# Attention and feed-forward: products with V in other places of a batch's second group, and zero products in the last two batches

## The chip, the cores and the metric

The kernel runs on one core of a Trainium2 chip. The time is device microseconds of one execution, and the number compared is the median of several. Five engines work side by side: TensorE (PE; its weight loads are PEld), VectorE (DVE), ScalarE (ACT), GpSimd (POOL) and SyncE (SP), which here only issues DMAs. Each runs its own list of instructions in order and waits on semaphores for the others. TensorE's clock has two levels, 2.4 GHz and 1.2 GHz; the profile gives what was granted as a share, 1.00 or 0.50.

## The reference

A post-norm transformer block over x of 8 batches, 512 tokens, 128 channels, fp32:

```python
qkv = x @ w_qkv                      # (8, 512, 384); 16 heads of 8 channels
att = einsum('bhtd,bhsd->bhts', q, k) / sqrt(8)
att = softmax(where(causal, att, -inf))
x = layernorm(x + einsum('bhts,bhsd->bhtd', att, v))
h = silu(x @ wg.T) * (x @ wu.T)      # 384 hidden, weights are integers / 127
x = layernorm(x + h @ wd.T)
```

## The kernel before, in words

The work has an attention stage, up to about 320 us, and a feed-forward stage behind it, which the change does not touch.

**Groups.** The attention stage runs over 32 groups of four heads, four groups a batch, numbered G = 0 to 31. TensorE's list is written out by hand: `group0` to `group3`, called for G = 4b+1 to 4b+4. So `group1`, the "second group" of batch b in this text, holds G = 4b+2. Three groups are in flight in each of these functions:

- `scores(G, s)`, five steps: K times Q for keys at or before the query, into one of two pairs of PSUM banks (line 449, 35 rows of the array). ScalarE takes each pair away with one exp (`exp_slot`, line 707) into `pt`, GpSimd clears the part above the diagonal (line 935).
- `maxima(M, k)`, for the group M = G + 2, two steps at a time, k = 0, 2, 4, 6, 8: Q times K into one of three banks (line 466, 33 rows), from which VectorE takes each row's maximum (line 792). GpSimd splits these (line 923), `turn_negmax` transposes them (line 431), ScalarE copies them, a DMA puts them beside Q.
- `values(V, ...)`, for the group V = G - 1: the exps times V, in five pieces (line 489). The products are fp32 with all 128 rows of the array and 32 of its columns, four heads one after the other into the four quarters of bank `pv_ps`. A piece is named by its block of keys: "0a" and "0b" are 256 queries each, "1" is 384, "2" is 256, "3" is 128. One piece is four products in the code and eight records in the profile. Two groups share the bank; when the second is complete, ScalarE copies it to `oT` (`copy_out`, line 721), and `turn_out` transposes it in the next group.

**Projections.** Batch b + 2's projections of q and k (line 405, 512 columns, fp32) stand in `group1`, b + 1's projection of V (line 421) in `group0`. They use the same two pairs of PSUM banks as the scores. ScalarE copies their results (`copy_q_or_k`, line 686), GpSimd splits them, and DMAs lay them out for the scores of a later batch. So `group1` of batches 6 and 7 has no projection of q and k, and `group0` of batch 7 none of V.

**Order of the banks.** `SCORE_TURNS` and `MAXIMA_TURNS` list who takes a pair or a bank in turn; a step waits until the one two (or three) turns before it has been read.

**Zeros.** `keep_busy(n)` runs n products of a tile of zeros, bf16, 512 columns (line 498), into `pv_ps` while nothing is in it, in the start of the kernel alone.

Of the kernel before, what the change touches and what calls it, by code (L numbers as in the profile page):

```python
# [32 lines left out]
P = 128  # L33
B, T, C = 8, 512, 128
# [91 lines left out]
def attention_ffn(nc, x, w_qkv, w_gate, w_up, w_down, out):  # L126
    ctx = ExitStack()
    with ctx:
        def sb(name, shape, dt):
            return ctx.enter_context(nc.sbuf_tensor(name, shape, dt))  # L130
# [7 lines left out]
        pv_ps = psum[:, 7, :]  # L138
# [18 lines left out]
        zeros = sb("zeros", [P, T], BF16)  # L157
# [225 lines left out]
        def _(pe):  # L383
# [23 lines left out]
            def project_q(b):  # L407
                if b < B:
                    project(b, 0, take_pair("Q", b)[:, 0, :])
# [5 lines left out]
            def project_v(b):  # L415

                if b < B:
                    pair = take_pair("VX", b)
                    pe.wait_ge(xt_copied, b + 1)
                    for n in range(NB):  # L420
                        last = pe.matmul(pair[:, 0, C * n:C * n + C], xT[:, P * n:P * n + P], wqkv[:, 2 * C:3 * C],  # L421
                                         start=True, stop=True)
                    last.then_inc(v_made, 1)
                    if b + 1 < B:
                        turn_x(b + 1, pair[:, 1, :])
# [29 lines left out]
            def maxima(M, k):  # L455

                if M < GROUPS:
                    u, g = M // NG % 2, M % NG
                    if k == 0:
                        pe.wait_ge(qk_loaded[u][g], LOADED * (M // NG // 2 + 1))  # L460
                    for k in (k, k + 1):
                        bank, at = take_bank("M", M, k), 64 * (k % 2)
                        blocks = max_blocks(k)
                        for n, (hh, i, col) in enumerate(blocks):
                            width = P * (i + 1)
                            last = pe.matmul(bank[:, col:col + width],  # L466
                                             qx[u][at:at + KM, 2 * g + hh // 2, P * i:P * i + P].bitcast(F32R),
                                             kx[u][at:at + KM, 2 * g + hh // 2, 0:width].bitcast(F32R),
                                             start=(n == 0), stop=(n == len(blocks) - 1), skip_group_check=True)
                        last.then_inc(mx_full, 1)  # L470

            def values(G, *pieces):


                u, g = G // NG % 2, G % NG
                half, par = g // 2, g % 2
                for piece in pieces:
                    j = int(piece[0])
                    first, last_q = (0, 256) if piece[1:2] == "a" else (256, T) if piece[1:2] == "b" else (P * j, T)
                    if piece == "0a":  # L480
                        if g == 0:
                            pe.wait_ge(v_copied, G // NG + 1)
                        if par == 0 and G > 1:
                            pe.wait_ge(ot_copied, G // 2)
                    pe.wait_ge(diag_done, NB * G + (1, 2, 4, 3)[j])
                    for hh in range(HG):
                        bank, col = key_block_place(hh, j)
                        at = (j * H + 8 * half + 2 * hh + par) * VW + (VW // 2) * (1 - par)
                        last = pe.matmul(pv_ps[VW * hh:VW * hh + VW, first:last_q], vx[u][:, at:at + VW],  # L489
                                         pt[g % 2][:, bank, col + first - P * j:col + last_q - P * j],  # L490
                                         start=(piece == "0a" and par == 0), stop=False, skip_group_check=True)
                    last.then_inc(pv_piece, 1)

            def keep_busy(n):


                for _ in range(n):
                    pe.matmul(pv_ps, zeros[:, 0:P], zeros[:], start=True, stop=True, skip_group_check=True)  # L498

            def first_maxima(M):  # L500
                for k in range(0, MX, 2):
                    maxima(M, k)
                    if M > 0 and k == 0:
                        turn_negmax(0)
                    keep_busy(3)
# [11 lines left out]
            def group0(G):  # L517
                V, M, b = G - 1, G + LAG, G // NG
                scores(G, 0)
                scores(G, 1)  # L520
                values(V, "0a")
                maxima(M, 0)
                values(V, "1", "0b")
                turn_negmax(G + 1)
                maxima(M, 2)
                scores(G, 2)
                turn_out(half_of(G))
                scores(G, 3)
                maxima(M, 4)
                values(V, "2", "3")  # L530
                scores(G, 4)
                maxima(M, 6)
                project_v(b + 1)
                maxima(M, 8)

            def group1(G):
                V, M, b = G - 1, G + LAG, G // NG
                values(V, "0a")
                scores(G, 0)
                scores(G, 1)  # L540
                maxima(M, 0)
                values(V, "1", "0b", "2")
                maxima(M, 2)
                turn_negmax(G + 1)
                scores(G, 2)
                values(V, "3")
                maxima(M, 4)
                scores(G, 3)
                maxima(M, 6)
                project_q(b + 2)  # L550
                scores(G, 4)
                maxima(M, 8)
                project_k(b + 2)

# [112 lines left out]
        def _(act):  # L667
# [34 lines left out]
            def exp_slot(G, s):  # L702
                if G < GROUPS:
                    act.wait_ge(st_full, SLOTS * G + s + 1)
                    if G > 1:
                        act.wait_ge(pv_piece, PIECES * (G - 2) + pieces_read(G - 2, s))
                    act.activation(pt[G % 2][:, 2 * s:2 * s + 2, :], pair_of("S", G, s), ACT.Exp,  # L707
                                   scale=SM_SCALE).then_inc(exp_done, 1)
# [26 lines left out]
            for G in range(GROUPS + 1):  # L735
                b, n = (G - 1) // NG, (G - 1) % NG
                exp_slot(G, 0)
                exp_slot(G, 1)
                copy_negmax(G + 1)
                exp_slot(G, 2)  # L740
                if n == 1:
                    copy_out((G - 2) // 2)
                exp_slot(G, 3)
                if n == 1 and G > 0:
                    copy_q_or_k(b + 2, 0)
                exp_slot(G, 4)
                if n == 0:
                    copy_v_and_x(b + 1)
                if n == 1:
                    copy_q_or_k(b + 2, 1)  # L750
                if n == 3 and G > 0:
                    copy_out((G - 2) // 2)
# [285 lines left out]
```

## Time and profile before

| | us |
|---|---|
| median of 3 runs | 402.44 |
| the three runs | 421.72, 396.28, 402.44 |
| the profiled execution's own time | 399.73 |
| its span, first to last instruction | 398.0 |
| mean granted clock of TensorE in it | 0.888 |
| TensorE busy | 361.3 (91%) |
| VectorE busy | 290.0 (73%) |
| ScalarE busy | 215.1 (54%) |
| GpSimd busy | 186.6 (47%) |

The profile is of one execution, and its times are set against 399.73, not against the median. A busy share says how long an engine had an instruction in it; a matmul at the lower clock is busy for longer with the same work, so busy time and clock have to be read together.

### The profile page before, as it was taken

How to read it: one execution, taken by the hardware profiler on the slowest of the kernel's cores; microseconds unless marked ns; L12 is line 12 of the kernel's file. 1: busy time of each engine (PE TensorE's matmuls, PEld its weight loads, DVE VectorE, ACT ScalarE, POOL GpSimd, SP SyncE). 2: the span in 40 equal slices, each digit the busy share in tenths (PEclk: the TensorE clock that was granted, in tenths of full speed). 3: DMA queues.
4: the chain of work that ended last, by engine and by line, in shares of the span. 5: the costliest groups of instructions: out<-in, count | busy, mean ns of one | idle time of the engine just before them, and what ended most of it. 6: DMA issues, size and time to landing. Idle time of an engine off the chain costs nothing.

```text
span 398.0 us, 9029 instructions
## 1 busy us (share of the span) xinstructions
PE 361.3 (91%) x2900; PEld 207.4 (52%) x2900; DVE 290.0 (73%) x1239; ACT 215.1 (54%) x277; POOL 186.6 (47%) x349
## 2 busy tenths in 40 slices
PE   5598999999999999999999999999999869788781
PEld 3233465446556445555565564565455437667661
DVE  6777656798898745788888988898587125776751
ACT  3301636586876644667868767776476733332220
POOL 8300312644553461247445525644234455787854
PEclk9969558799999755899999999999599787999998
DMA  5895301174156214433641661543000000001001
GB/s 161 276 321 169 107 3 55 50 259 126 54 217 200 68 62 155 118 119 112 222 132 30 237 194 31 212 152 94 3 4 4 28 2 0 28 28 53 28 27 54
DMA packets 33903, 41.74 MB, mean 105 GB/s; under 512 B 3136, under 2 KB 17472, under 8 KB 33856
## 3 DMA queue, kind: packets, MB, share of 16 engines
q1 hardware_dynamic: 33856, 41.17, 31.8%
q8 instruction: 23, 0.38, 0.4%
q14 instruction: 24, 0.20, 0.2%
HBM read 21.76 MB, written 18.87 MB: 102 GB/s over the span
## 4 chain that ended last, share of the span: by engine, by line
PE 71%; DVE 10%; POOL 6%; issue 6%; DMA 3%; ACT 2%; SPq 0%; POOLq 0%; DVEq 0%; ACTq 0%
PE psum L489 21%; PE psum L466 17%; PE psum L449 13%; PE psum L405 5%; PE psum L396 4%; DVE masked L792 4%; POOL x L994 3%; PE psum L498 2%; PE psum L431 2%; PE psum L421 2%; PE psum L648 2%; POOL rstd L983 2%; DVE stats L846 2%; DMA scr_k<-parts 1%; DVE nm L792 1%
## 5 line engine op out<-in xcount | busy, mean ns | idle before, releaser
L792 DVE CUSTOM_DVE_ANT_0 masked<-psum,mask 128x384 bf16<-128x384 f32 (+3 forms) x512 | 219.7, 487 | 57.7 <-PE psum L466 49.9
L707 ACT ACTIVATE pt<-psum 128x1024 f32<-128x1024 f32 x160 | 158.6, 1022 | 67.3 <-PE psum L449 66.4
L935 POOL TENSOR_SCALAR_AFFINE_SELECT pt<-pt 128x512 f32<-128x512 f32 x128 | 79.6, 634 | 125.7 <-ACT pt L707 124.2
L466 PE MATMUL psum<-kx,qx 33*128 33x384 f32 (+3 forms) x512 | 100.8, 383 | 6.4 <-DMA kx<-scr_k 2.9
L489 PE MATMUL psum<-pt,vx 128*32 128x256 f32 (+2 forms) x1280 | 100.8, 424 | 0.3 <-POOL pt L935 0.3
L449 PE MATMUL psum<-qx,kx 35*128 35x384 f32 (+3 forms) x512 | 83.5, 375 | 1.3 <-ACT pt L707 1.3
L466 PEld LDWEIGHTS psum<-kx,qx 33*128 33x128 f32 x512 | 58.7, 206 | 47.2 <-DVE nm L792 22.5
L449 PEld LDWEIGHTS psum<-qx,kx 35*128 35x128 f32 x512 | 51.4, 209 | 34.5 <-issue 20.9
L489 PEld LDWEIGHTS psum<-pt,vx 128*32 128x32 f32 x1280 | 32.9, 115 | 42.9 <-issue 29.4
L792 DVE DVE_READ_ACCUMULATOR2_ANT nm<- 128x1 f32 x512 | 42.5, 83 | 0.0
L923 POOL TENSOR_SCALAR nm_parts<-nm 128x16 fp32r<-128x16 f32 x32 | 6.6, 206 | 55.2 <-DVE nm L792 54.5
L766 ACT ACTIVATE sg<-psum 128x512 f32<-128x512 f32 x24 | 14.3, 596 | 29.4 <-PE psum L639 28.6
L715 ACT ACTIVATE nm_T<-psum 32x128 f32<-32x128 f32 x32 | 8.5, 266 | 35.9 <-PE psum L431 35.9
L648 PE MATMUL psum<-wT,pt 128*128 128x128 f32 x192 | 22.9, 276 | 1.5 <-DVE pt L881 1.5
L648 PEld LDWEIGHTS psum<-wT,pt 128*128 128x128 f32 x192 | 22.5, 192 | 2.8 <-DVE pt L881 2.3
L405 PE MATMUL psum<-xT,wqkv 128*128 128x512 f32 x32 | 22.2, 796 | 1.6 <-ACT xT L674 1.6
L636 PE MATMUL psum<-x_hi,wT 128*128 128x512 f32 x48 | 22.0, 459 | 0.7 <-ACT x_hi L758 0.7
L639 PE MATMUL psum<-x_lo,wT 128*128 128x512 f32 x48 | 21.0, 437 | 1.7 <-DVE x_lo L862 1.7
L881 DVE TENSOR_TENSOR pt<-psum,sg 128x512 f32<-128x512 f32 x24 | 16.0, 670 | 3.6 <-PE psum L639 2.8
L983 POOL TENSOR_TENSOR rstd<-veps,minus_half 128x4 f32<-128x4 f32 x16 | 16.1, 1009 | 0.0
L954 POOL TENSOR_TENSOR parts<-full,parts 128x512 fp32r<-128x512 f32 x12 | 15.4, 1283 | 1.0
L1005 POOL TENSOR_SCALAR yo<-r,minus_mean,rstd 128x128 f32<-128x128 f32 x32 | 13.9, 448 | 2.0 <-POOL rstd L983 2.0
(60 smaller groups left out, 272.5 us busy)
## 6 DMA issues: line engine op xcount, KB each, us to landing
scr_q<-parts SPq DMA_DIRECT2D x16, 512.0 KB, 3.6
scr_k<-parts SPq DMA_DIRECT2D x16, 512.0 KB, 5.4
qx<-scr_q SPq DMA_DIRECT2D x64, 128.0 KB, 2.5
kx<-scr_k SPq DMA_DIRECT2D x64, 128.0 KB, 2.6
xa<-L_attn_x SPq DMA_DIRECT2D x8, 256.0 KB, 3.2
res<-L_attn_x SPq DMA_DIRECT2D x8, 256.0 KB, 2.7
out<-yo SPq DMA_DIRECT2D x8, 256.0 KB, 2.2
qx<-nm_T SPq DMA_DIRECT2D x64, 8.0 KB
```

Source lines behind the costliest of these rows:

```text
L405: pe.matmul(dst, wqkv[:, C * n:C * n + C], xT[:], start=True, stop=True).then_inc((q_made, k_made)[n], 1)
L449: last = pe.matmul(pair[:, bank % 2, col:col + width], kx[u][at:at + KS, 2 * g + hh // 2, P * j:P * j + P].bitcast(F32R), qx[u][at:at + KS ...
L466: last = pe.matmul(bank[:, col:col + width], qx[u][at:at + KM, 2 * g + hh // 2, P * i:P * i + P].bitcast(F32R), kx[u][at:at + KM, 2 * g + ...
L489: last = pe.matmul(pv_ps[VW * hh:VW * hh + VW, first:last_q], vx[u][:, at:at + VW], pt[g % 2][:, bank, col + first - P * j:col + last_q - ...
L636: pe.matmul(psum[:, bank + k % 2, :], w, x1_hi[u][:].bitcast(F32R), start=True, stop=False)
L639: pe.matmul(psum[:, bank + k % 2, :], w, x1_lo[u][:].bitcast(F32R), start=False, stop=True).then_inc(full, 1)
L648: last = pe.matmul(psum[:, 5, C * n:C * n + C], hid[u][:, m, P * n:P * n + P], wT[:, 2, P * m:P * m + P], start=(m == 0 and n == 0), stop= ...
L707: act.activation(pt[G % 2][:, 2 * s:2 * s + 2, :], pair_of("S", G, s), ACT.Exp, scale=SM_SCALE).then_inc(exp_done, 1)
L792: dve.tensor_tensor_reduce(masked[count % 4][:, 0:width], bank[:, col:col + width], mask[:, T - width:T], -1.0, 3.0e38, ALU.add, ALU.min, ...
L881: dve.tensor_tensor(hid[u][:, m, :], psum[:, 3 + k % 2, :], sg[k % 2][:], ALU.mult).then_inc(hid_made, 1)
L935: pool.affine_select(out=blocks, in_=blocks, pattern=[[0, HG], [1, P]], compare_op=ALU.is_ge, fill=0.0, base=0, channel_multiplier=-1).the ...
L983: pool.tensor_tensor(rstd[:, k, :], veps[:, k, :], minus_half[:], ALU.pow).then_inc(rstd_made, 1)
```

## The change

In `group1`, piece "2" of the products with V no longer follows piece "0b" at once but stands behind `scores(G, 2)`, and piece "3" moves from there to behind `scores(G, 3)`. ScalarE's copy of the completed sums moves behind the exp of step 3 to match. In batch 6, whose `group1` has no projection, piece "3" stands behind `scores(G, 4)` and the copy behind the exp of step 4; four products of zeros are added to the open sums of `pv_ps` behind `maxima(M, 6)`. In `group0` of batch 7, which has no projection of V, four more stand behind `maxima(M, 6)`. They are written with start and stop off, so they add nothing to what is in the bank. No product of the computation is dropped or added.

```diff
--- before.py
+++ after.py
@@ -497,6 +497,11 @@
                 for _ in range(n):
                     pe.matmul(pv_ps, zeros[:, 0:P], zeros[:], start=True, stop=True, skip_group_check=True)
 
+            def add_zeros(n):
+
+                for _ in range(n):
+                    pe.matmul(pv_ps, zeros[:, 0:P], zeros[:], start=False, stop=False, skip_group_check=True)
+
             def first_maxima(M):
                 for k in range(0, MX, 2):
                     maxima(M, k)
@@ -530,6 +535,8 @@
                 values(V, "2", "3")
                 scores(G, 4)
                 maxima(M, 6)
+                if b + 1 == B:
+                    add_zeros(4)
                 project_v(b + 1)
                 maxima(M, 8)
 
@@ -539,16 +546,23 @@
                 scores(G, 0)
                 scores(G, 1)
                 maxima(M, 0)
-                values(V, "1", "0b", "2")
+                values(V, "1", "0b")
                 maxima(M, 2)
                 turn_negmax(G + 1)
                 scores(G, 2)
-                values(V, "3")
+                values(V, "2")
                 maxima(M, 4)
                 scores(G, 3)
-                maxima(M, 6)
-                project_q(b + 2)
-                scores(G, 4)
+                if b + 2 == B:
+                    maxima(M, 6)
+                    add_zeros(4)
+                    scores(G, 4)
+                    values(V, "3")
+                else:
+                    values(V, "3")
+                    maxima(M, 6)
+                    project_q(b + 2)
+                    scores(G, 4)
                 maxima(M, 8)
                 project_k(b + 2)
 
@@ -738,12 +752,14 @@
                 exp_slot(G, 1)
                 copy_negmax(G + 1)
                 exp_slot(G, 2)
-                if n == 1:
+                exp_slot(G, 3)
+                if n == 1 and b + 2 != B:
                     copy_out((G - 2) // 2)
-                exp_slot(G, 3)
                 if n == 1 and G > 0:
                     copy_q_or_k(b + 2, 0)
                 exp_slot(G, 4)
+                if n == 1 and b + 2 == B:
+                    copy_out((G - 2) // 2)
                 if n == 0:
                     copy_v_and_x(b + 1)
                 if n == 1:
```

TensorE, `group1` of batches 0 to 5, before. L489 with 32x384 is piece "1", with 32x256 x8 pieces "0b" and "2", with 32x128 piece "3"; L466 are maxima, L449 scores, L431 the transposed maxima, L405 the projection of q:

```order
L489 MATMUL psum<-pt,vx 32x384 x4
L489 MATMUL psum<-pt,vx 32x256 x8
L466 MATMUL psum<-kx,qx 128x512 x2
L431 MATMUL psum<-identf,nm_parts 128x128
L449 MATMUL psum<-qx,kx 128x384
...
L489 MATMUL psum<-pt,vx 32x128 x4
L466 MATMUL psum<-kx,qx 128x384
...
L449 MATMUL psum<-qx,kx 128x384
...
L466 MATMUL psum<-kx,qx 128x384
...
L405 MATMUL psum<-xT,wqkv 128x512
```

Pieces "1", "0b" and "2" stand in one burst, and the single piece "3" in all that follows up to the projection. The same place in TensorE's list now:

```order
L489 MATMUL psum<-pt,vx 32x384 x4
L489 MATMUL psum<-pt,vx 32x256 x4
L466 MATMUL psum<-kx,qx 128x512 x2
L431 MATMUL psum<-identf,nm_parts 128x128
L449 MATMUL psum<-qx,kx 128x384
...
L489 MATMUL psum<-pt,vx 32x256 x4
L466 MATMUL psum<-kx,qx 128x384
...
L449 MATMUL psum<-qx,kx 128x384
...
L489 MATMUL psum<-pt,vx 32x128 x4
L466 MATMUL psum<-kx,qx 128x384
...
L405 MATMUL psum<-xT,wqkv 128x512
```

Eight products became four in the burst; "2" (32x256) stands where "3" was, and "3" (32x128) a scores step later, ahead of maxima 6 and the projection.

TensorE, `group1` of batch 6 from the piece behind scores 2 to piece "0a" of the next group, before:

```order
L489 MATMUL psum<-pt,vx 32x128 x4
L466 MATMUL psum<-kx,qx 128x384
...
L449 MATMUL psum<-qx,kx 128x384
...
L466 MATMUL psum<-kx,qx 128x384
...
L449 MATMUL psum<-qx,kx 128x256 x4
L466 MATMUL psum<-kx,qx 128x256 x4
L466 MATMUL psum<-kx,qx 128x512 x2
L449 MATMUL psum<-qx,kx 128x512 x2
L489 MATMUL psum<-pt,vx 32x256 x4
```

After piece "3" come scores and maxima alone up to the next L489. The same place in TensorE's list now; L503 are the zero products:

```order
L489 MATMUL psum<-pt,vx 32x256 x4
L466 MATMUL psum<-kx,qx 128x384
...
L449 MATMUL psum<-qx,kx 128x384
...
L466 MATMUL psum<-kx,qx 128x384
...
L503 MATMUL psum<-zeros 128x512 x4
L449 MATMUL psum<-qx,kx 128x256 x4
L489 MATMUL psum<-pt,vx 32x128 x4
L466 MATMUL psum<-kx,qx 128x256 x4
L466 MATMUL psum<-kx,qx 128x512 x2
L449 MATMUL psum<-qx,kx 128x512 x2
L489 MATMUL psum<-pt,vx 32x256 x4
```

In that stretch "2" stands at its head, four zero products ahead of scores 4 (L449 with 128x256) and "3" behind them.

ScalarE, a `group1` of batches 0 to 5: L707 are exps, L715 the copy of the transposed maxima, L721 the copy of the V sums, L686 the copies of q and k, before:

```order
L707 ACTIVATE pt<-psum 128x1024 x2
L715 ACTIVATE nm_T<-psum 32x128
L707 ACTIVATE pt<-psum 128x1024
L721 ACTIVATE oT<-psum 128x512
L707 ACTIVATE pt<-psum 128x1024
L686 ACTIVATE full<-psum 128x512
L707 ACTIVATE pt<-psum 128x1024
L686 ACTIVATE full<-psum 128x512
```

The copy to oT stands between two exps. The same place in ScalarE's list now (the lines are L721, L729, L735 and L700):

```order
L721 ACTIVATE pt<-psum 128x1024 x2
L729 ACTIVATE nm_T<-psum 32x128
L721 ACTIVATE pt<-psum 128x1024 x2
L735 ACTIVATE oT<-psum 128x512
L700 ACTIVATE full<-psum 128x512
L721 ACTIVATE pt<-psum 128x1024
L700 ACTIVATE full<-psum 128x512
```

The copy of the sums has moved behind the exp of step 3 and stands right ahead of q's copy.

## Rows read from the trace of the kernel before

**Rows 1.** The page: busy time of each engine, and the granted clock in 40 slices.

```profile
PE 361.3 (91%) x2900; PEld 207.4 (52%) x2900; DVE 290.0 (73%) x1239; ACT 215.1 (54%) x277; POOL 186.6 (47%) x349
...
PEclk9969558799999755899999999999599787999998
```

**Rows 2.** Windows, one a batch: length, engines' busy us (records), clock, DMA share, GB/s.

```profile
61.76:97.23 35.47, 35.11 (x321) 18.74 (x324) 28.85 (x134) 24.10 (x31) 15.36 (x28) 0.90 0.42 137
97.23:129.87 32.64, 32.30 (x322) 18.07 (x324) 28.71 (x134) 24.00 (x31) 16.58 (x29) 1.00 0.46 148
129.87:173.31 43.44, 43.27 (x321) 22.46 (x324) 29.24 (x134) 24.32 (x31) 16.59 (x29) 0.69 0.34 112
...
206.07:238.73 32.66, 32.33 (x320) 18.06 (x324) 28.70 (x134) 24.01 (x31) 16.58 (x29) 1.00 0.43 140
238.73:270.93 32.20, 31.88 (x316) 17.67 (x320) 28.69 (x134) 23.49 (x30) 16.57 (x29) 1.00 0.42 141
270.93:306.45 35.52, 33.98 (x302) 18.19 (x306) 28.54 (x133) 21.64 (x27) 12.83 (x25) 0.86 0.04 12
```

**Rows 3.** Windows over the stretches at the lower clock; columns as in rows 2.

```profile
66.90:73.70 6.80, 6.80 (x24) 2.15 (x23) 3.98 (x19) 3.28 (x5) 4.05 (x7) 0.50 0.26 76
135.20:162.40 27.20, 27.18 (x158) 12.91 (x156) 15.38 (x71) 12.65 (x15) 11.01 (x19) 0.50 0.37 125
278.50:288.70 10.20, 10.20 (x68) 4.64 (x65) 5.90 (x25) 4.24 (x5) 2.29 (x5) 0.50 0.01 3
39.60:60.00 20.40, 20.40 (x117) 11.81 (x115) 11.26 (x52) 10.31 (x13) 5.41 (x10) 0.50 0.18 55
```

**Rows 4.** Timeline of TensorE, batch 2: start, us, line, operation, shapes, records, [idle before].

```profile
129.80 1.72 PE L489 MATMUL psum<-pt,vx 128*32 128x384 f32 x24
...
134.30 0.50 PE L466 MATMUL psum<-kx,qx 33*128 33x384 f32 x2 [0.16 <-DVE nm L792]
134.73 1.70 PE L405 MATMUL psum<-xT,wqkv 128*128 128x512 f32 x2
```

**Rows 5.** Windows of line 489 alone (products with V): length, PE, PEld, clock.

```profile
63.44:66.68 3.24, 0.43 (x8) 0.16 (x8) 1.00 0.02 5
...
240.38:243.60 3.22, 0.43 (x8) 0.16 (x8) 1.00 0.02 5
...
272.58:278.95 6.37, 0.43 (x8) 0.16 (x8) 0.97 0.16 44
```

**Rows 6.** The chain that ended last: start, us, what.

```profile
35.18 0.75 PE psum L498 x3
...
206.07 1.65 PE psum L489 x24
```

**Rows 7.** Timelines of TensorE and VectorE, single steps.

```profile
40.40 0.61 PE L498 MATMUL psum<-zeros 128*128 128x512 bf16 x1
...
103.91 1.12 PE L405 MATMUL psum<-xT,wqkv 128*128 128x512 f32 x2
...
208.18 0.69 DVE L792 CUSTOM_DVE_ANT_0 masked<-psum,mask 128x512 bf16<-128x512 f32 x1 [0.67 <-PE psum L466]
...
267.87 1.16 PE L421 MATMUL psum<-wqkv,xT 128*128 128x128 f32 x8
```

**Rows 8.** Timeline of ScalarE, second group of batch 4.

```profile
209.81 0.59 ACT L721 ACTIVATE oT<-psum 128x512 f32<-128x512 f32 x1
210.37 1.02 ACT L707 ACTIVATE pt<-psum 128x1024 f32<-128x1024 f32 x1
212.09 0.60 ACT L686 ACTIVATE full<-psum 128x512 f32<-128x512 f32 x1 [0.70 <-PE psum L405]
```

**Rows 9.** Timeline of TensorE, batches 6 and 7: waits for VectorE.

```profile
276.74 0.50 PE L466 MATMUL psum<-kx,qx 33*128 33x256 f32 x2 [0.19 <-DVE nm L792]
...
304.71 0.50 PE L466 MATMUL psum<-kx,qx 33*128 33x256 f32 x2 [0.23 <-DVE nm L792]
```

**Rows 10.** Timeline of TensorE, second group of batch 7.

```profile
311.41 0.50 PE L449 MATMUL psum<-qx,kx 35*128 35x512 f32 x2 [0.99 <-ACT pt L707]
```

## The prediction

> **What bounds the kernel now.** I read the page first. TensorE is busy 91% of the 398.0 us span, VectorE 73% [rows 1]. The line of the granted clock is not flat: it dips near its fifth digit, in the middle and again near the end of the attention stage [rows 1]. The time is therefore TensorE's, at two levels of its clock, 2.4 GHz and 1.2 GHz, and the reader should ask where each is granted.
>
> Then I cut the attention stage into batches, from the first product with V behind the second group's first maxima to the same place a batch later [rows 2]. Batches 1, 3 and 4 ran at clock 1.00; the first of them took 32.64 us and the last 32.66, with TensorE busy 32.3. Batch 0 took 35.47 at a mean clock of 0.90, batch 2 took 43.44 at 0.69: the same instructions. Batch 6, whose projections are missing, took 35.52 at 0.86, where it should be shorter than batch 5 (32.20). The low stretches stand at 0.50, that is 1.2 GHz: 66.9 to 73.7, 135.2 to 162.4 and 278.5 to 288.7 us, and one before the batches, 39.6 to 60.0 [rows 3]. TensorE is busy through nearly all of them, so a low clock is paid in full.
>
> What did TensorE do before each fall? In batch 2, 24 records of products with V (fp32, 128 rows of the array each) end at 131.5; then come score and maxima products, which use 33 or 35 rows, and only the eight records of piece "3" until the projection at 134.73, which already runs into the low clock (1.70 us) [rows 4]. The view of line 489 alone puts a number on it: in the 3.2 us from the end of that burst to the projection V products are busy 0.43 us. That stretch stands six times, in batches 0 to 5, with the same work each time (first and last of the six in [rows 5]); two of the six ended in a fall. In batch 6, with no projection to close it, it is 6.37 us long, again with 0.43 us of V work, and the clock falls inside it [rows 5]. So all three falls go with one stretch of the program, the one poorest in V products; whether the clock falls there was chance in batches 0 to 5 and, in the longer stretch of batch 6, hardly is.
>
> Here a rule speaks against the change. TensorE was idle only 0.16 us before the fall of batch 2 [rows 4]. The Trainium skill, "TensorE: Matmul & The Clock Gate", section "HAM oscillation — how this bites in real kernels", has the clock drop when the array sits idle between bursts, and its advice is to avoid idle gaps. By that rule batches 0 and 2 fell for a reason that an order of busy products doesn't touch. The row disagrees, since the array was never idle long; what the rule would make of the time is the third rival below.
>
> **The change, part by part.**
>
> *Batches 0 to 5, second group.* TensorE gets the same products in another order. Piece "2" moves out of the burst to behind scores 2, piece "3" from there to behind scores 3. The stretch of 3.2 us then holds pieces "2" and "3". Piece "2" has 256 columns where "3" has 128; a burst of 896 columns takes 1.65 us on the chain [rows 6], so "2" is 256/896 of it, 0.47, and the V work of the stretch goes from 0.43 to about 0.9 us, in two places instead of one. I expect no fall there. What it frees, against a batch at full clock (32.66): batch 0 gives 35.47 - 32.66 = 2.8, batch 2 gives 43.44 - 32.66 = 10.8 us. Bounds: 0 each if falls remain, the whole 13.6 if none does. I take the whole.
>
> Side effect on VectorE: now it waits 0.67 us at the burst for maxima [rows 7], and then TensorE waits 0.16 us for it just before the projection [rows 4]. With a shorter burst maxima 2 and 4 come some 0.4 us earlier, maxima 6 at the same time. The TensorE wait should go: 0.15 us in six batches, 0.9 us. Bounds: 0 and 1.0.
>
> *ScalarE.* The copy of the V sums moves behind exp 3. Today exp 3 starts right behind that copy (209.81 + 0.59, then 210.37), and the copy of q starts at 212.09 after 0.70 us idle, since it waits for the projection [rows 8]. Exchanging the two leaves their common end where it is; piece "3", for which the copy now waits, is done 0.4 us after scores 3, inside exp 3 (1.02 us). Cost 0. If that cover went, q's copy would come up to 0.6 us late, and scores 4, the projection of k, the parts on GpSimd and their DMAs behind it; these last are wanted a batch later. In batch 6 the copy stands behind exp 4 and nothing but two maxima steps and scores 0 of the next group (about 1.8 us on TensorE) covers exp 4's rest and 0.6 us of copy, before piece "0a" may start. I price that at 0, with 0.3 as the bad end.
>
> *Zero products, batches 6 and 7.* Two sets of four. At full clock three such products take 0.75 us on the chain, 0.25 each [rows 6]; at the low clock one is recorded with 0.61 us [rows 7]. Eight cost 2.0 us if nothing hides them. For batch 6 without a fall I start from batch 5's 32.20, take off two projections of 1.12 and one of V at 1.16 [rows 7], which leaves 28.8, and add 2.0: 30.8. VectorE has 28.54 us of work in this stretch [rows 2], so it isn't the bound but it is close: TensorE waited 35.52 - 33.98 = 1.5 us in it, waits on VectorE as at 276.74 [rows 9]. If these waits stay beside the zero products the stretch is 32.3 and the gain 3.2; if the zero products fall wholly into waits it is about 29.5, gain 6.0. I take 31.0, gain 4.5, because the four in batch 6 stand just where TensorE waits for VectorE, and those in batch 7 where a wait of 0.23 us was the only one near [rows 9].
>
> *Batch 7, second group.* Its scores wait for ScalarE (0.99 us idle at 311.41) [rows 10]. Scores 2 come half a microsecond sooner with the shorter burst, so the row of exps starts sooner: 0.4 us, bounds 0 and 0.5.
>
> **Sum**, against the profiled execution's own 399.73 us: 399.7 - 2.8 - 10.8 - 0.9 - 4.5 - 0.4 = 380.3. That execution lies 2.7 us below the median of the three runs shown, so against 402.44 it is 5.5% faster. The feed-forward stage and the low stretch before the batches are not touched and stay in.
>
> **Rivals.**
>
> *One fall remains.* Of six stretches one still ends in a fall. A fall costs 2.8 to 10.8, so the time is 383 to 391. For it: the V work of the stretch is doubled, but it still is the poorest stretch. Against: with 0.43 us only two of six fell.
>
> *Zeros don't hold the clock.* Batches 0 to 5 behave as forecast, batch 6 falls anyway: 399.7 - 2.8 - 10.8 - 0.9 - 0.4 + 2.0 = 386.8. For it: the low stretch 39.6 to 60.0 went on while zero products ran (the one at 40.40) [rows 3, 7].
>
> *It doesn't do what it says.* The falls have another cause than the order of busy products. Then the time is 399.7 - 0.9 - 0.4 + at most 2.0 = 400.4, some 399 if half of the zero products are hidden. This is the idle-gap rule's case. Against it: all three falls stand at one and the same place of the program.
>
> *Slower.* The burst of 24 is also the densest V work of a batch. If the clock is low when a batch begins, that burst may be what lifts it, and the change breaks it up. Price: batch 2 lost 10.8 us in 27.2 us of low clock, so work runs there at 16.4/27.2 = 0.60 of its pace, and a batch low throughout takes 54 us, 21 more. One such batch brings 380 to 401, two bring 423; the change is slower from the second on. For it: the clock is low until 60.0 [rows 3], just before the first burst, that of [rows 2]'s first stretch. Against: none of the rises in these rows follows that burst; the one at 60.0 and the one at 73.7 stand elsewhere.
>
> **How the numbers follow.** Chances: forecast 0.58 (380; its own range 373 to 386, with the low start of 20.4 us at 0.60 pace worth up to 8 us should it be shorter another time); one fall remains 0.17; zeros don't hold 0.05; not what it says 0.09; slower 0.11, of which 0.04 with one batch. The range 373 to 395 leaves out the last two, 0.20. A measurement tells 2% from nothing here, since the runs before differ by more than that among themselves. Faster by over 2% (below 394.4) takes the first three, 0.80; within 2% takes 0.09 + 0.04 = 0.13; slower 0.07.
>
> **What the profile after would show.** Right: every batch 0 to 5 about 32.5 us at clock 1.00; batch 6 near 31 at 1.00; V busy about 0.9 us between burst and projection; no wait of 0.16 before the projection; the zero products at 0.25 each. Wrong: a low stretch that begins at a second group's projection, low clock in batch 6 behind the zero products, or a whole batch near 54 us. The prediction fails most easily on chance: how long the clock stays low once it has fallen (6.8 or 27.2 us) is something this profile shows but doesn't explain.

## The result

| | median us | executions |
|---|---|---|
| kernel before | 402.44 (396.28 to 421.72) | 5 |
| changed kernel | 377.86 (375.56 to 395.15) | 5 |

The ratio is 0.946, with a 95% interval from 0.932 to 0.961. Ratios and their intervals, here and below, are taken over the fast executions of each kernel alone. How far the executions of one kernel lie apart turned out to be part of the subject, so for the changed kernel, which also ran twice more among the experiments, I give all 17 executions: median 382.0, from 375.2 to 395.5, five of them between 395.0 and 395.5.

The execution profiled first is one of those five: 395.15 us, span 393.4. Its page, the lines that answer to [rows 1]:

```profile
PE 360.6 (92%) x2908; PEld 205.9 (52%) x2908; DVE 289.6 (74%) x1239; ACT 214.8 (55%) x277; POOL 186.7 (47%) x349
...
PEclk9955556999999999999999999997558888999997
```

The dip in the middle of the attention stage is gone, one near its end has stayed, and the one at the start is longer. The windows from one second group to the next, columns as in [rows 2] (length, busy us of PE, PEld, DVE, ACT, POOL, clock, DMA share, GB/s):

```profile
66.60:99.05 32.45, 32.22 (x319) 17.98 (x317) 28.79 (x133) 24.04 (x31) 15.37 (x28) 1.00 0.46 150
99.05:131.48 32.43, 32.24 (x318) 17.97 (x317) 28.70 (x133) 24.03 (x31) 16.55 (x29) 1.00 0.46 149
...
228.88:260.88 32.00, 31.81 (x315) 17.58 (x313) 28.71 (x133) 23.55 (x30) 16.55 (x29) 1.00 0.43 139
260.88:303.57 42.69, 41.73 (x309) 20.89 (x307) 28.84 (x133) 21.84 (x27) 12.87 (x25) 0.68 0.04 12
```

Batches 0 to 5 each take 32.0 to 32.5 us at clock 1.00; their sum, from 66.60 to 260.88, is 194.28 us, where it was 209.17, from 61.76 to 270.93 [rows 2]. Batch 6 is the other way: 42.69 at 0.68 against 35.52. The two stretches at the lower clock in this part of the trace, same columns:

```profile
20.80:65.10 44.30, 42.90 (x181) 20.04 (x181) 25.91 (x118) 11.89 (x15) 6.27 (x14) 0.50 0.44 130
269.90:297.20 27.30, 27.28 (x175) 13.15 (x171) 15.40 (x70) 12.57 (x16) 6.66 (x14) 0.50 0.01 2
```

The first of them lies wholly before the batches, in code that the change leaves alone, and in this execution the first burst starts 4.8 us later (66.60 against 61.76). The second is batch 6's fall.

TensorE's timeline, batch 0, answers to [rows 4] (start, us, line, operation, shapes, records, idle before):

```profile
66.60 1.28 PE L489 MATMUL psum<-pt,vx 128*32 128x384 f32 x16
...
68.93 0.64 PE L489 MATMUL psum<-pt,vx 128*32 128x256 f32 x8
...
70.43 0.43 PE L489 MATMUL psum<-pt,vx 128*32 128x128 f32 x8
70.78 0.59 PE L466 MATMUL psum<-kx,qx 33*128 33x384 f32 x4
71.31 1.13 PE L405 MATMUL psum<-xT,wqkv 128*128 128x512 f32 x2
```

The burst is 16 records instead of 24; piece "2" (256 columns) and piece "3" (128) stand one behind each of scores 2 and 3; maxima 6 at 70.78 has no wait in front of it, where 0.16 us stood. The view of the V line alone, between burst and projection, answers to [rows 5]:

```profile
67.88:71.38 3.50, 1.07 (x17) 0.32 (x16) 1.00 0.04 10
```

1.07 us of V work in 3.5, against 0.43 in 3.2. VectorE and ScalarE in the second group of batch 1, which answer to [rows 7] and [rows 8]:

```profile
100.80 0.69 DVE L808 CUSTOM_DVE_ANT_0 masked<-psum,mask 128x512 bf16<-128x512 f32 x1 [0.23 <-PE psum L466]
...
102.50 0.56 DVE L808 CUSTOM_DVE_ANT_0 masked<-psum,mask 128x384 bf16<-128x384 f32 x1 [0.39 <-PE psum L466]
```

```profile
102.98 1.02 ACT L721 ACTIVATE pt<-psum 128x1024 f32<-128x1024 f32 x1 [0.46 <-PE psum L449]
103.90 0.59 ACT L735 ACTIVATE oT<-psum 128x512 f32<-128x512 f32 x1
104.92 0.60 ACT L700 ACTIVATE full<-psum 128x512 f32<-128x512 f32 x1 [0.43 <-PE psum L405]
```

VectorE's wait of 0.67, behind which stood a second one of 0.17 in the kernel before,

```profile
209.66 0.56 DVE L792 CUSTOM_DVE_ANT_0 masked<-psum,mask 128x384 bf16<-128x384 f32 x1 [0.17 <-PE psum L466]
```

has become one of 0.23, and the second has grown to 0.39: 0.62 us together instead of 0.84. ScalarE's copy of the sums (103.90) stands behind the fourth exp, and the copy of q behind it still waits 0.43 us for the projection: the exchange is covered. Last, batch 6, in TensorE's timeline, which answers to [rows 9]:

```profile
265.15 0.50 PE L466 MATMUL psum<-kx,qx 33*128 33x384 f32 x2 [0.30 <-DVE nm L808]
265.59 1.04 PE L503 MATMUL psum<-zeros 128*128 128x512 bf16 x4
...
266.99 0.43 PE L489 MATMUL psum<-pt,vx 128*32 128x128 f32 x8
...
268.71 0.50 PE L466 MATMUL psum<-kx,qx 33*128 33x512 f32 x1 [0.65 <-DVE nm L808]
```

Four zero products take 1.04 us; behind them come scores 4, piece "3" and a wait of 0.65 us for VectorE ahead of the maxima at 268.71, and the clock falls at 269.9, when piece "0a" of the next group has just run.

### The profile page after: what moved, and what is told of

It is laid out like the page before. It is cut to its first block, busy times and chain, and to the rows that moved or that the text cites. A ratio compares the mean times of both kernels' runs of the same rounds, so it can differ in the third digit from the quotient of the medians.

```text
span 393.4 us, 9045 instructions
## 1 busy us (share of the span) xinstructions
PE 360.6 (92%) x2908; PEld 205.9 (52%) x2908; DVE 289.6 (74%) x1239; ACT 214.8 (55%) x277; POOL 186.7 (47%) x349
## 4 chain that ended last, share of the span: by engine, by line
PE 74%; DVE 9%; POOL 6%; issue 5%; DMA 3%; ACT 2%; SPq 0%; POOLq 0%; DVEq 0%; ACTq 0%
PE psum L489 21%; PE psum L466 19%; PE psum L449 14%; PE psum L405 4%; PE psum L498 4%; PE psum L396 4%; POOL x L1010 3%; DVE masked L808 2%; PE psum L431 2%; PE psum L421 2%; PE psum L662 2%; POOL rstd L999 2%; DVE stats L862 2%; DMA scr_k<-parts 1%; DVE pt L897 1%
## 5 line engine op out<-in xcount | busy, mean ns | idle before, releaser
L721 ACT ACTIVATE pt<-psum 128x1024 f32<-128x1024 f32 x160 | 158.6, 1022 | 69.1 <-PE psum L449 68.4
L466 PE MATMUL psum<-kx,qx 33*128 33x384 f32 (+3 forms) x512 | 97.7, 387 | 4.4 <-DMA kx<-scr_k 2.4
L489 PE MATMUL psum<-pt,vx 128*32 128x256 f32 (+2 forms) x1280 | 100.2, 417 | 0.3 <-POOL pt L951 0.3
L449 PE MATMUL psum<-qx,kx 35*128 35x384 f32 (+3 forms) x512 | 81.1, 367 | 1.1 <-DMA qx<-nm_T 0.8
L466 PEld LDWEIGHTS psum<-kx,qx 33*128 33x128 f32 x512 | 56.8, 208 | 45.4 <-issue 22.0
L449 PEld LDWEIGHTS psum<-qx,kx 35*128 35x128 f32 x512 | 49.4, 203 | 32.8 <-issue 17.8
L489 PEld LDWEIGHTS psum<-pt,vx 128*32 128x32 f32 x1280 | 31.9, 114 | 42.0 <-issue 29.0
L782 ACT ACTIVATE sg<-psum 128x512 f32<-128x512 f32 x24 | 14.3, 596 | 29.1 <-PE psum L653 27.5
L729 ACT ACTIVATE nm_T<-psum 32x128 f32<-32x128 f32 x32 | 8.5, 266 | 34.8 <-PE psum L431 34.8
L405 PE MATMUL psum<-xT,wqkv 128*128 128x512 f32 x32 | 19.2, 697 | 1.7 <-ACT xT L688 1.6
L498 PE MATMUL psum<-zeros 128*128 128x512 bf16 x43 | 19.0, 562 | 0.0
```

The lines of the kernel that those rows point to most:

```text
L405: pe.matmul(dst, wqkv[:, C * n:C * n + C], xT[:], start=True, stop=True).then_inc((q_made, k_made)[n], 1)
L449: last = pe.matmul(pair[:, bank % 2, col:col + width], kx[u][at:at + KS, 2 * g + hh // 2, P * j:P * j + P].bitcast(F32R), qx[u][at:at + KS ...
L466: last = pe.matmul(bank[:, col:col + width], qx[u][at:at + KM, 2 * g + hh // 2, P * i:P * i + P].bitcast(F32R), kx[u][at:at + KM, 2 * g + ...
```

## The experiments

All are written against the kernel before or the changed one. Medians are over all executions of a kernel; the kernel before, on the same chips, had medians of 402.8, 403.8, 400.4 and 403.2 us in the four sets.

**1. All pieces in the burst.** In `group1` of the kernel before:

```diff
-                values(V, "1", "0b", "2")
+                values(V, "1", "0b", "2", "3")
                 maxima(M, 2)
                 turn_negmax(G + 1)
                 scores(G, 2)
-                values(V, "3")
```

> The kernel before with piece "3" pulled forward too, so that all pieces but "0a" stand in one burst in each second group and no V product lies between the burst and the projection of q. If the falls go with the V-poor stretch, it now falls in more batches than the two of six seen before: each further fall costs 2.8 to 10.8 us, so about 410 to 420 us. If the falls have another cause, TensorE's work and busy time are the same and the time stays near 402.

Measured: 404.5 us (392.7 to 419.1, 6 executions), before 402.8. The windows of the two batches that fell (batch 0 took 32.66):

```profile
90.65:137.12 46.47, 46.25 (x318) 23.36 (x316) 29.21 (x133) 24.33 (x31) 16.61 (x29) 0.63 0.32 103
...
202.56:245.97 43.41, 43.19 (x319) 22.56 (x317) 29.21 (x133) 24.33 (x31) 16.62 (x29) 0.69 0.34 109
```

Two of six again, not more. Taking the last 0.43 us of V work out of the stretch made no difference that these executions can tell: the forecast of 410 to 420 missed, and by the words put down beforehand a time near 402 spoke for another cause than the poor stretch. It may be that once the stretch is poor, poorer changes little, but no run shows that. What weighs against this result is the next pair.

**2 and 3. Zero products in the stretch, with 128 rows or with 32.** The kernel before, and one line more in `group1` of batches 0 to 5; in the third experiment `add_zeros` takes only the first 32 rows of the tile.

```diff
                 scores(G, 2)
+                if b + 2 < B:
+                    add_zeros(3)          # 128 rows; experiment 3: 32 rows
                 values(V, "3")
```

> The kernel before with three zero products (128 rows, 512 columns, bf16) added to the open sums behind scores 2 of the second group of batches 0 to 5; V pieces stay where they were and batch 6 is not treated. They cost 6 x 0.75 = 4.5 us at full clock. If full-height work in the stretch holds the clock, batches 0 to 5 no longer fall: 402 - 13.6 + 4.5 = about 393, with batch 6's fall still there. If the place of the V pieces matters for another reason, nothing is won: about 406.

> The same three zero products in the same place, with 32 rows of the array instead of 128: as long on TensorE, no idle time more or less. If it is the rows at work that the falls go with, the falls of batches 0 to 5 stay: about 402 + 4.5 = 406 to 407. If it is busy time, or idle gaps, it does what the 128-row version does: equal to it, about 393.

Measured: 394.1 us (387.2 to 401.8, 8 executions) with 128 rows, 420.8 (403.3 to 425.5, 6 executions) with 32, beside 402.8 for the kernel before. The ratio of the first to before is 0.986, interval 0.969 to 1.003, so against the kernel before a gain isn't clear of noise; against each other the two versions don't overlap, 401.8 at most and 403.3 at least. The zero products of both and the wait behind them, from TensorE's timelines, first with 128 rows:

```profile
161.96 0.82 PE L502 MATMUL psum<-zeros 128*128 128x512 bf16 x3
...
164.44 0.50 PE L466 MATMUL psum<-kx,qx 33*128 33x384 f32 x2 [0.30 <-DVE nm L798]
```

and with 32 rows:

```profile
158.72 0.82 PE L502 MATMUL psum<-zeros 32*128 32x512 bf16 x3
...
161.19 0.76 PE L466 MATMUL psum<-kx,qx 33*128 33x384 f32 x2 [0.29 <-DVE nm L798]
```

Each trio takes 0.82 us, and the idle time ahead of the last maxima is 0.30 and 0.29: TensorE is as busy in one as in the other. The windows with 128 rows (batches 3, 5 and 6; batches 0, 1, 2 and 4 have 33.39 to 33.43):

```profile
159.19:192.71 33.52, 33.04 (x322) 18.04 (x320) 28.80 (x133) 24.15 (x31) 16.60 (x29) 1.00 0.45 143
...
226.12:259.11 32.99, 32.53 (x317) 17.87 (x316) 28.71 (x133) 23.67 (x30) 16.59 (x29) 1.00 0.43 138
259.11:301.83 42.72, 42.14 (x301) 21.49 (x299) 28.72 (x133) 21.75 (x27) 12.85 (x25) 0.64 0.04 10
```

and with 32 rows (batches 2 to 5; batches 0 and 1 have 33.37 and 33.41):

```profile
122.55:155.95 33.40, 32.92 (x322) 18.27 (x320) 28.72 (x133) 24.16 (x31) 16.60 (x29) 1.00 0.45 145
155.95:196.69 40.74, 40.04 (x322) 20.69 (x320) 29.14 (x133) 24.38 (x31) 16.62 (x29) 0.79 0.37 119
196.69:243.88 47.19, 46.88 (x321) 23.45 (x319) 29.23 (x133) 24.47 (x31) 16.62 (x29) 0.64 0.30 97
243.88:287.62 43.74, 43.43 (x318) 22.25 (x316) 29.24 (x133) 24.01 (x30) 16.62 (x29) 0.69 0.32 104
```

With 128 rows none of batches 0 to 5 falls, with 32 rows three do, in a row, each at the projection. This is the experiment that decides: same order, same busy time of the zeros, same waits, and only the height of the zero products differs. It shows this for products of zeros; that the spread pieces work by their height too is carried over from it, since no run spreads work of fewer rows. The 32-row zeros cost 18 us over the kernel before, not the 4.5 forecast. In this profile that is one more fall than the two of before, and longer ones; why zeros of 32 rows should be worse than none isn't shown. The falls lie at

```profile
161.40:178.20 16.80, 16.80 (x83) 7.33 (x83) 9.27 (x43) 6.76 (x9) 7.87 (x12) 0.50 0.28 97
202.30:236.20 33.90, 33.88 (x194) 15.42 (x192) 19.15 (x90) 15.33 (x19) 12.49 (x22) 0.50 0.30 101
250.10:277.20 27.10, 27.09 (x158) 12.90 (x156) 15.32 (x71) 12.67 (x15) 10.71 (x19) 0.50 0.32 108
```

**4. The spread alone.** The changed kernel without the eight zero products.

```diff
-                if b + 1 == B:
-                    add_zeros(4)
                 project_v(b + 1)
...
                     maxima(M, 6)
-                    add_zeros(4)
                     scores(G, 4)
```

> The changed kernel without its eight zero products. If the spread accounts for batches 0 to 5 and the zeros for batch 6, batches 0 to 5 stay at 32.4 us each and batch 6 falls in every execution: 378 - 2.0 for the zero products + 5 to 12 for the fall = 381 to 388. If the zero products do nothing, 376 to 378.

Measured: 392.5 us (384.3 to 395.4, 6 executions), ratio to before 0.976, interval 0.959 to 0.992. Batch 4 and batch 6 in its windows:

```profile
196.32:228.75 32.43, 32.25 (x319) 17.96 (x317) 28.70 (x133) 24.03 (x31) 16.59 (x29) 1.00 0.45 147
...
260.74:303.49 42.75, 42.00 (x301) 21.35 (x299) 28.73 (x133) 21.86 (x27) 12.83 (x25) 0.64 0.04 10
```

Batches 0 to 5 are as in the changed kernel (32.42, 32.44, 32.43, 32.54, 32.43, 31.99), and batch 6 falls in the profiled execution; of the others only the times are known. The spread by itself is worth about 10 us of the medians. The median is 4.5 us above the forecast's upper end. The base of that forecast, 378, was the median of five executions; over 17 it is 382.0.

**5. The changed kernel again**, for a profile in which batch 6 does not fall.

> The changed kernel as it is, for more executions of it and a profile in which batch 6 doesn't fall. By the reading that its zero products mostly hold the clock in batch 6, most executions lie at 375 to 382 us and a few at 395, as in the five seen; batch 6 takes about 31 us where the clock holds.

Measured: 384.4 us (375.7 to 395.5, 6 executions, two at 395.5). The profiled one took 382.3, with batches 0 and 6 as follows:

```profile
63.27:95.69 32.42, 32.19 (x319) 17.95 (x317) 28.77 (x133) 24.03 (x31) 15.38 (x28) 1.00 0.47 150
...
257.52:289.33 31.81, 30.40 (x306) 16.49 (x306) 28.32 (x133) 21.62 (x27) 12.88 (x25) 1.00 0.05 15
```

and behind its zero products, in TensorE's timeline:

```profile
265.35 0.50 PE L466 MATMUL psum<-kx,qx 33*128 33x512 f32 x1 [0.63 <-DVE nm L808]
...
266.02 0.64 PE L489 MATMUL psum<-pt,vx 128*32 128x256 f32 x8
```

Batch 6 at full clock takes 31.81 us; TensorE waits 31.81 - 30.40 = 1.4 us in it, about what it waited before. The wait ahead of the next group is VectorE's, and piece "0a" behind it (266.02) starts with none: the copy of the sums behind exp 4 holds nobody up.

**6. The zero products alone.** The kernel before with the zero products of batches 6 and 7 (and piece "3" and the copy of batch 6 moved behind scores 4, so that the sums are open):

```diff
                 scores(G, 2)
-                values(V, "3")
+                if b + 2 != B:
+                    values(V, "3")
                 maxima(M, 4)
                 scores(G, 3)
                 maxima(M, 6)
+                if b + 2 == B:
+                    add_zeros(4)
                 project_q(b + 2)
                 scores(G, 4)
+                if b + 2 == B:
+                    values(V, "3")
...
```

The four zero products in batch 7's `group0` and the place of ScalarE's copy are as in the changed kernel.

> The kernel before with the zero products of batches 6 and 7 alone (and piece "3" and the copy of batch 6 behind scores 4 so that the sums are open); the pieces of batches 0 to 5 stay in the burst. If the two halves of the change are independent, batches 0 to 5 still fall here and there and batch 6 no longer always: 402.5 less 5 to 12 = 390 to 398 us. If the zeros need the spread, 402.

Measured: 400.3 us (392.8 to 420.5, 12 executions), ratio 1.000, interval 0.989 to 1.011.

```profile
96.63:142.92 46.29, 46.11 (x319) 23.41 (x317) 29.21 (x133) 24.33 (x31) 16.60 (x29) 0.63 0.32 103
...
175.54:211.15 35.61, 35.29 (x319) 18.60 (x317) 28.88 (x133) 24.11 (x31) 16.55 (x29) 0.90 0.42 135
...
243.79:278.89 35.10, 34.77 (x314) 18.42 (x312) 28.80 (x133) 23.61 (x30) 16.55 (x29) 0.90 0.39 131
278.89:310.74 31.85, 30.52 (x306) 16.61 (x307) 28.30 (x133) 21.63 (x27) 12.87 (x25) 1.00 0.04 13
```

Batches 1, 3 and 5 fall, batch 6 doesn't (31.85). In this profile the zero products do in batch 6 what they should, but the median lies above the 390 to 398 that I had for independent halves, and near the 402 of the other case: alone the zeros bring 3.5 us of the medians (not clear of noise), on top of the spread some 10 (392.5 to 382.0, not all on one chip). Why the halves don't add up isn't shown.

**7. Without batch 7's zero products.**

```diff
-                if b + 1 == B:
-                    add_zeros(4)
```

> The changed kernel without the four zero products of batch 7. The profile before never fell in that place, and four products cost 1.0 us at most: equal to the changed kernel, 377 to 378 us, or 1 less. If batch 7's four matter for the clock, 380 or more.

Measured: 381.0 us (377.2 to 395.0, 6 executions, one at 395.0), against 384.4 for the changed kernel on the same chip. Its batch 6, which ends behind the place where the four stood:

```profile
258.48:290.23 31.75, 30.12 (x303) 16.48 (x302) 28.28 (x133) 21.63 (x27) 12.86 (x25) 1.00 0.05 13
```

31.75 against 31.81 with them: they cost 0.06 us in these two profiles, so they hide in waits. The median is above the 380 that I had put down as a sign that they matter, but so is that of the changed kernel with them, so no execution shows that they are needed.

**8. Six zero products in batch 6, and "3" behind them.** The changed kernel with

```diff
                     maxima(M, 6)
-                    add_zeros(4)
+                    add_zeros(3)
                     scores(G, 4)
+                    maxima(M, 8)
+                    add_zeros(3)
                     values(V, "3")
-                maxima(M, 8)
```

> The changed kernel with six zero products in batch 6's second group instead of four, three behind maxima 6 and three behind maxima 8, and piece "3" behind these, so that the stretch in which the profiled execution fell at 269.9 has full-height work at its head. It costs 0.5 us more. If that stretch is why some executions lie at 395, they go, and the median stays at 376 to 379 with a highest under 385. If not, the highest stays at 395.

Measured: 375.4 us (374.0 to 381.5, 6 executions), ratio to before 0.942, interval 0.934 to 0.949. Batch 6, and the second trio with piece "3" behind it:

```profile
256.92:288.22 31.30, 30.48 (x308) 16.41 (x308) 28.40 (x133) 21.74 (x27) 12.87 (x25) 1.00 0.05 16
```

```profile
263.06 0.82 PE L503 MATMUL psum<-zeros 128*128 128x512 bf16 x3
263.81 0.43 PE L489 MATMUL psum<-pt,vx 128*32 128x128 f32 x8
```

No execution at 395, and batch 6 takes 31.30, half a microsecond less than with four: TensorE is idle 0.8 us in it (31.30 - 30.48) instead of 1.4. The edit changes the number of zero products and the place of three of them and of piece "3" together; which of the two counts isn't separated.

**9 and 10. The start.** Two edits on top of experiment 8, one each, aimed at the low stretch before the batches.

```diff
-            keep_busy(8)
+            keep_busy(18)        # experiment 9: while K and Q are loaded
...
-                    keep_busy(3)
+                    keep_busy(1)         # experiment 10: behind each maxima step of the start
```

> The kernel of the run before this (six zero products in batch 6, three behind maxima 8) with 18 zero products instead of 8 at the start, in the 2 to 3 us in which TensorE waits for the first rows of K and Q, just before its clock falls at about 20 us. If full-height work holds the clock there too, the low stretch of some 35 us before the batches gets shorter: at 0.6 of the pace it is worth up to 14 us, some 5 to 10 of it to be won, so 366 to 371 us. If the fall comes later at the groups before the batches anyway, 375.

> The same kernel as the last with one zero product instead of three behind each of the ten maxima steps at the start. In the profiles these run at the low clock at 0.45 us each: 20 fewer save up to 9 us if TensorE is what the start waits for, 366 us. If they are what ends the low clock later, or VectorE takes over, the same 375 or a few us more.

Measured: 374.5 us (370.2 to 379.1, 6 executions) and 378.7 (373.1 to 389.1, 8 executions); kernel before 400.4 in this set. The stretch from 15 to 60 us in experiments 8, 9 and 10, in this order:

```profile
15.00:60.00 45.00, 41.05 (x189) 18.09 (x190) 28.71 (x121) 11.94 (x17) 5.41 (x13) 0.62 0.50 153
```

```profile
15.00:60.00 45.00, 41.46 (x218) 20.84 (x219) 29.92 (x131) 13.20 (x19) 6.26 (x14) 0.73 0.51 154
```

```profile
15.00:60.00 45.00, 39.74 (x218) 20.05 (x218) 33.09 (x141) 15.02 (x21) 7.36 (x17) 0.66 0.50 154
```

With the longer filling the clock there is 0.73 against 0.62, the first fall comes at 28.8 us instead of about 20, and another at 42.5. But that isn't shown to be the filling's doing, for experiment 2, whose start is as in the kernel before, has the same 0.73 and its first fall at 29.1:

```profile
15.00:60.00 45.00, 41.14 (x225) 19.32 (x227) 31.55 (x137) 13.91 (x19) 6.71 (x16) 0.73 0.50 154
```

Of the 5 to 10 us expected about 1 is left in the median, no difference that can be told. The version with fewer zeros has an earlier first burst in its profile (57.24 us against 62.71) and no better median; I can't say why.

**11 and 12. The changed kernel and version 8 side by side, again.**

> The changed kernel once more, beside the version with six zero products in batch 6, on one chip, because the two medians so far (382.0 over eleven executions against 375.4 over six) lie closer than single executions of the changed kernel do. If batch 6 still falls in a part of its executions, about one in four lies at 395 and the median at 378 to 385.

> The version with six zero products in batch 6 and piece "3" behind them once more. If they hold the clock there, no execution lies at 395 again and the median is 374 to 378, below the changed kernel's of the same chip by 3 to 8 us. If the first six were luck, it looks like the changed kernel.

Measured on one chip: changed 385.2 us (375.2 to 395.3, 6 executions, two at 395), version 8 376.3 (373.8 to 384.5, 7 executions), kernel before 403.2. Together with the earlier sets the changed kernel lies at 395 in 5 of 17 executions, version 8 in 0 of 13, with medians of 382.0 and 376.3. Experiments 9 and 10 have version 8's batch 6 too, and none of their 14 executions lies at 395 either (the highest is 389.1); their profiled ones and experiment 12's held the clock in batch 6.

## Why the prediction was right

The forecast was 380.3 us, the median first measured 377.9 and the one over all 17 executions 382.0. By its steps, in the profile of experiment 5, whose batch 6 did not fall (span 380.5 against 398.0):

- *Batches 0 to 5.* Forecast 13.6 us for the falls and 0.9 for VectorE's wait, 14.5 together. From 63.27 to 257.52 it is 194.25 us against 209.17: 14.9 less. Falls in these stretches, over all the profiles: 10 of 24 with the burst and at most 32-row zeros (before, experiments 1, 3, 6), 0 of 60 with the spread or with 128-row zeros (the profile after, experiments 2, 4, 5 and 7 to 12). The wait is gone; a batch at full clock went from 32.66 to about 32.43, 0.2 instead of 0.15.
- *V work in the stretch.* Forecast 0.9 us, measured 1.07.
- *ScalarE's copy.* Forecast 0. q's copy still waits 0.43 us for the projection, and piece "0a" of batch 6 does not wait.
- *Zero products and batch 6.* Forecast 4.5 us, from 35.52 to 31.0. Where the clock held, 35.52 to 31.81, 3.7: TensorE's waits of 1.4 us stayed beside the zeros instead of taking them in, near the bad end that I had put at 32.3.
- *Batch 7 and the rest.* Forecast 0.4. From batch 7's mark to the end it is 91.17 us (380.5 - 289.33) against 91.55 (398.0 - 306.45): 0.4.

The sum of these is 14.9 + 3.7 + 0.4 = 19.0, less 1.5 us for a later first mark (63.27 against 61.76): 17.5, which is 398.0 - 380.5.

The term that was mis-sized is that of the zero products. I priced batch 6's fall at what the one profile showed, some 4.5 us, and took the zeros to end it always. A fall in batch 6 costs 42.7 - 31.8 = 10.9 us in the profile after and in experiment 4, and it did not always go: batch 6 fell in all five profiles without zeros in it (before, experiments 1 to 4), in one of five with the four of the change (the profile after; not in experiments 5, 6, 7 and 11) and in none of four with six (experiments 8, 9, 10 and 12). In the medians the four are worth about 10 us on top of the spread (392.5 without, 382.0 with). The spread's 14.5 in turn is what the profile before had lost; in the medians it is 10.3 (402.8 to 392.5).

How often the four zeros fail is known only roughly. Five of 17 executions lie where the profiled one with its fall lay. Without a fall in batch 6 the latest first burst seen (66.6), 194.3 us for batches 0 to 5, 31.8 for batch 6 and 91.2 for the rest give a span of 383.9, and with the 1.7 us by which an execution's own time exceeds its span, 385.6. The two at 386.5 and 389.6 lie above that, among the times of experiment 4 (384.3 to 395.4), so the estimate is five to seven of 17; no trace shows those two.

That the number came out so near is partly luck. Errors of 4 and 6 us in opposite directions nearly cancel in the sum. The 19.4 us were taken off an execution of 399.73; off the median of 402.44 they give 383.0. The first median, 377.9, came from five executions with one at 395, and lies 4 us below that of all 17.

Of the rivals, "one fall remains" spoke of batches 0 to 5, and no profile with the spread has a fall there. What did happen in part of the executions is "zeros don't hold the clock": batches 0 to 5 as forecast, and batch 6 falls anyway, as in the very execution profiled first, at 395.15 and not at the 386.8 that I had for it. Its reason was wrong, since products of zeros did hold the clock in experiment 2 and in batch 6 most of the time; it is the step from "zeros count" to "so batch 6 never falls" that failed. The second half of that stretch, from the zeros to piece "0a", was left poor, and no execution of version 8, which puts three more there, lies at 395.

The rule on idle gaps (the Trainium skill, "TensorE: Matmul & The Clock Gate", "HAM oscillation — how this bites in real kernels") does not account for these falls: experiments 2 and 3 have the same gaps and the same busy time, and 394 against 421 us. The rival that rested on it, 399 us, is out. Of the slow rival nothing was seen: in no profile did the clock stay low through a spread burst and a whole batch after it.

The prediction's list of low stretches is not complete. It ties the three falls that it names behind the start to the stretch behind a second group's burst. The clock in the kernel before was also low from 312.7 to 319.4 us, in batch 7, and from 326.3 to 333.1, where the feed-forward stage starts. In batch 7 it falls under the changed kernel too, though the pieces are spread there as well (the kernel before, then experiment 5):

```profile
312.70:319.40 6.70, 6.70 (x50) 3.35 (x48) 1.94 (x10) 3.32 (x4) 2.39 (x4) 0.50 0.00 0
```

```profile
295.70:302.20 6.50, 6.50 (x52) 3.35 (x48) 1.95 (x10) 2.86 (x4) 1.85 (x3) 0.51 0.00 0
```

In experiment 5 the V products are busy 1.94 of the 4.95 us from the end of batch 7's burst to that fall, a larger share than the 1.07 of 3.5 at which batches 0 to 5 held, and TensorE waits 0.80 us once. So the share of V work alone doesn't say where the clock falls. The profiles of experiments 8 and 10 have no fall there and take 88.6 and 88.7 us from batch 7's mark to the end, those of experiments 5, 7, 9, 11 and 12 have one and take 90.8 to 91.2: some 2.5 us that neither the change nor the forecast touches.

What stays open: how long the clock remains low once it has fallen. 6.8, 10, 17, 27 and 34 us all occur in the batches, and batch 6 with the same order of work took 35.5 us in the kernel before and 42.7 in experiment 2. The start's low stretches vary from execution to execution too, and with them the first mark. With the same list of work ahead of it, it stands at 55.8 to 64.0 us in the five profiles with the burst (before, experiments 1, 2, 3 and 6) and at 61.9 to 66.6 in the seven with the spread (the profile after, experiments 4, 5, 7, 8, 11 and 12). Whether that is chance or a price of the change, these profiles don't tell.

## What to carry to other kernels

Where TensorE is busy throughout and the granted clock still falls, look for the stretch of the program that most falls have in common, list the falls that stand elsewhere too, and look at what the products there use of the array's rows. Here, moving full-height products into it cost nothing in a batch, and products of zeros into an open sum cost 0.25 us each, or nothing where TensorE waited anyway. Run the kernel several times and read the executions one by one: a median and one profile hide that a fall happens in five or so of seventeen. Look at what follows the filler too: in the execution profiled first the clock fell 3.3 us behind the four zeros.

## What the runs showed of the hardware

Three bf16 products of zeros, 128 rows by 512 columns, held the clock at 1.00 in six of six stretches; with the same three at 32 rows it fell in three of six, at the same 0.82 us of TensorE time. That is one profile of each; the times of 8 and 6 executions (387.2 to 401.8, 403.3 to 425.5) go the same way. Once fallen, the clock stayed low although TensorE was busy: 27.28 of 27.30 us from 269.9 in the profile after. I had not expected zeros as data to count, nor the rows to matter that plainly. And a fall, once there, cost a batch between 2.8 us (35.47 against 32.66, before) and 13.8 (46.47 in experiment 1, against 32.66 for its batch 0).
